# Second layer's pairs: a step's lists behind its second product on TensorE, and the pair's sum ahead of the lists' sums on VectorE

## The reference

```
x = layernorm(x + attention0(x));  x = layernorm(x + experts0(x))    # 8 experts, each takes its 256 best tokens
x = layernorm(x + attention1(x));  x = layernorm(x + experts1(x))
def experts1(x):                   # w1: 16 experts x 512 x 128, w2: 16 x 128 x 512
    logits = -sum((x[:, :, None, :] - keys) ** 2, -1) + einsum('bld,ed->ble', x, rw) + rb
    topv, topi = top_k(logits, 4);  w = softmax(topv)
    hidden = gelu(einsum('bld,efd->blef', x, w1) + b1, approximate=False)
    exp_out = einsum('blef,edf->bled', hidden, w2) + b2
    return sum(w[..., None] * take_along_axis(exp_out, topi[..., None], axis=2), axis=2)
```

## Time and profile before

| | us |
|---|---|
| median of three runs | 627.19 (625.79 to 628.24) |
| the profiled execution, its own time | 627.36 |
| span of its trace | 625.5 |
| PE busy | 541.5 (87%) |
| ACT busy | 418.0 (67%) |
| DVE busy | 438.8 (70%) |
| POOL busy | 322.7 (52%) |

### The profile page before, as it was taken

How to read it: one execution, slowest core, us unless ns; L and a number is a source line. 1 busy time by engine, 2 the same in 40 slices (tenths; PEclk the granted TensorE clock), 3 DMA queues, 4 the chain that set the end, 5 groups by cost and what they waited for, 6 DMA issues and landing times.

```text
span 625.5 us, 16615 instructions
## 1 busy us (share of the span) xinstructions
PE 541.5 (87%) x5152; PEld 382.4 (61%) x5152; DVE 438.8 (70%) x1591; ACT 418.0 (67%) x1111; POOL 322.7 (52%) x429
## 2 busy tenths in 40 slices
PE   5579999999967995279999999987999999999960
PEld 2134444545755895244455544665899999999960
DVE  5478888994486521756799999497887788743275
ACT  2138888886261564163888988732778888899834
POOL 2675666506001678465144430646566777777740
PEclk9559999999999999575999999999999999999975
DMA  6602090002100225409405000102122211211363
GB/s 194 171 25 78 12 276 3 2 2 51 21 4 4 49 48 99 146 22 273 145 10 144 3 2 2 51 19 45 49 55 54 63 59 59 60 59 58 100 202 122
DMA packets 54649, 44.42 MB, mean 71 GB/s; under 512 B 15155, under 2 KB 45123, under 8 KB 54438
## 3 DMA queue, kind: packets, MB, share of 16 engines
q1 hardware_dynamic: 47302, 31.75, 17.6%
q0 software_dynamic: 7264, 11.62, 7.2%
HBM read 29.91 MB, written 11.87 MB: 67 GB/s over the span
## 4 chain that ended last, share of the span: by engine, by line
PE 67%; DVE 11%; DMA 5%; ACT 5%; issue 5%; SPq 3%; POOL 2%; DVEq 0%; ACTq 0%; POOLq 0%
PE bank L1321 11%; PE bank L1331 10%; PE bank L905 10%; PE bank L888 7%; PE bank L870 5%; PE bank L922 3%; ACT prob L1464 2%; PE bank L1116 2%; DVE W L1964 2%; PE bank L1128 2%; PE bank L946 2%; DMA sum<-rt,idx_s 1%; PE bank L1011 1%; PE bank L930 1%; DMA prob<-xs,idx_g 1%
## 5 line engine op out<-in xcount | busy, mean ns | idle before, releaser
L1771 DVE TENSOR_REDUCE mx<-bank 128x2 f32<-128x512 f32 x256 | 163.4, 686 | 38.2 <-PE bank L870 36.4
L1464 ACT ACTIVATE prob<-bank 128x512 f32<-128x512 f32 x256 | 142.1, 601 | 36.0 <-PE bank L888 31.2
L1650 ACT ACTIVATE queries<-bank,prob 128x128 f32<-128x128 f32 x316 | 90.1, 368 | 19.5 <-PE bank L1321 16.3
L1321 PE MATMUL bank<-keys,prob 128*128 x632 | 85.5, 279 | 0.7 <-issue 0.5
L1331 PE MATMUL bank<-W,queries 128*128 x632 | 84.4, 277 | 0.0
L870 PE MATMUL bank<-keys,queries 32*128 32x256 f16 x512 | 77.9, 293 | 4.2 <-DVE mx L1771 2.0
L905 PE MATMUL bank<-prob,augs 128*32 128x256 f32 x1024 | 79.0, 393 | 0.0
L1321 PEld LDWEIGHTS bank<-keys,prob 128*128 128x128 f32 x632 | 76.8, 192 | 3.4 <-issue 2.1
L784 POOL DMA_INDIRECT prob<-xs,idx_g x64 | 61.8, 966 | 32.6 <-DVE idx_g L2175 15.5
L1331 PEld LDWEIGHTS bank<-W,queries 128*128 128x128 f32 x632 | 76.7, 192 | 1.9 <-issue 0.5
L793 POOL DMA_INDIRECT parts<-augs,idx_s x64 | 63.0, 985 | 20.5 <-issue 8.9
(11 more groups left out here) (296 smaller groups left out, 1035.8 us busy)
## 6 DMA issues: line engine op xcount, KB each, us to landing
W<-in_w SPq DMA_DIRECT2D x48, 256.0 KB, 3.8
sum<-zero SPq DMA_DIRECT2D x3, 1024.0 KB, 9.8
xr<-XT SPq DMA_DIRECT2D x12, 128.0 KB, 2.0
xs<-X SPq DMA_DIRECT2D x2, 768.0 KB, 5.5
prob<-xs,idx_g POOLq DMA_INDIRECT x80, 2.6
XB<-sum SPq DMA_DIRECT2D x1, 1024.0 KB, 5.3
Y<-sum SPq DMA_DIRECT2D x4, 256.0 KB, 4.7
W<-sum SPq DMA_DIRECT2D x4, 256.0 KB, 5.4
```

The source lines that it names most:

```text
L1321: last = nc.tensor.matmul(bank[2 + p % 2][:, P * f:P * f + P], wc[:, p % 4, P * f:P * f + P], xsT2[:, bass.ds(at, 1), :], start=True, stop ...
L1464: nc.scalar.activation(prob[:, v % 8, :, :], st_bank(b, v)[:, :], ACT.Exp, scale=SCALE).then_inc(exp_done, 1)
L1650: last = nc.scalar.activation(hid2[:, p % 4, f, :], bank[2 + p % 2][:, P * f:P * f + P], ACT.Gelu, bias=wc[:, p % 4, WB + f:WB + f + 1])
L1771: nc.vector.tensor_reduce(m_at, bank[S1B[u % 2]][:, :].rearrange("p (j k) -> p j k", j=2), AX.X, ALU.max).then_inc(s1_used, 1)
```

## The change

On PE the lists of a step stand behind its second product, and no longer ahead of it. The wait of a list on `row_ready` is gone. The registers of the next pair (expert and slot) are asked for right behind the first product, ahead of the turns. On DVE the step begins with `row_owned`, the clearing, `pair_gated` and `pair_sum`, and then come `row_listed` and the next step's `row_indicator`.

```diff
             def row_list_of(t):
                 pe.wait_ge(row_ind, t + 1)
-                if t >= 2:
-                    pe.wait_ge(row_ready, t - 1)
                 nc.tensor.matmul(bank[4 + t % 2][:, 0:2 * P + 2], ind[:, t % 2, :], RH[:, :], start=True,
                                  stop=True).then_inc(row_list, 1)
-            def pair_first(e, p):
-                at = pair_slot(pe, e, p)
+            def pair_first(at, p):
                 pe.wait_ge(rows_in, min(p + 1, NJT[1]))
...
-                expert = {}
+                expert = {0: pair_expert(pe, words, 0)}
+                slot = {0: pair_slot(pe, expert[0], 0)}
                 for p in range(NPAIR + 2):
                     if p < NPAIR:
-                        expert[p] = pair_expert(pe, words, p)
-                        pair_first(expert[p], p)
+                        pair_first(slot.pop(p), p)
                     if p == 0:
                         fill(5)
+                    if p + 1 < NPAIR:
+                        expert[p + 1] = pair_expert(pe, words, p + 1)
+                        slot[p + 1] = pair_slot(pe, expert[p + 1], p + 1)
                     for t in TURNS[p]:
                         row_turn(t)
-                    for t in LISTS[p]:
-                        row_list_of(t)
                     if p < 2:
                         fill((6, 4)[p], 7)
                     if p >= 2:
                         pair_second(expert.pop(p - 2), p - 2)
+                    for t in LISTS[p]:
+                        row_list_of(t)
...
                 for p in range(NPAIR + 2):
-                    for t in LISTS[p]:
-                        row_listed(t)
-                    for t in LISTS[p + 1]:
-                        row_indicator(t)
                     for t in TURNS[p]:
                         row_owned(t)
                     if RING <= p + 1 < NJT[1]:
                         slot_cleared(p + 1)
                     if p >= 2:
                         e = pair_expert(dve, words, p - 2)
                         s = pair_slot(dve, e, p - 2)
                         pair_gated(e, s, p - 2)
                         pair_sum(s, p - 2)
+                    for t in LISTS[p]:
+                        row_listed(t)
+                    for t in LISTS[p + 1]:
+                        row_indicator(t)
                     if p == 3:
                         count_tiles()
```

## The result

| | before | after |
|---|---|---|
| median | 627.72 (4 runs, 625.79 to 629.25) | 635.68 (4 runs, 633.89 to 636.38) |
| ratio | | 1.012, 95% interval 1.0095 to 1.0145 |
| profiled execution, span | 627.36, 625.5 | 636.38, 634.5 |
| first product of pair 0 starts at | 435.10 | 437.02 |
| steps 2 to 16 | 33.94 | 36.91 |

So the change costs 8.0 us by the medians. The two profiled executions lie 9.0 apart, and 1.9 of that is there before the first pair starts, in a part of the program that is the same in both. The 64.57 of the earlier trace rows ends at a matmul start of 544.53, but the loads of that product start at 544.26, as the first matmul records are missing there; 64.31 is the better number, and the stretches of the experiments are taken from loads.

What follows compares the result with a forecast made beforehand. POOL's full queue of indirect DMAs from scatter 0 was taken to bound the kernel. PE's 8.6 us of lateness less 2.15 slack gave 6.4: 627.36 + 6.4 = 633.8, less 0.17 to the median, 633.6 us; range 627.0 to 637.5.

Steps and rivals of the forecast that it cites:

- The removed wait at 0: Dropping PE's row_ready wait ahead of each list: at most 0.21 us per list, taken as 0.
- That the registers are not fetched earlier: Next pair's registers on PE: the instructions stay directly at the first product despite the earlier text, so 0.
- The two-list loop: Steps 2 to 16, sum through lists to sum over two steps: 5.26 us a round, 36.8 against 33.94.
- The 0.2 us by which step 2 starts earlier: Step 2's second product on PE starts 0.2 us earlier, as its two lists no longer stand ahead of it.
- Nothing from step 16 to 18: Step 17 has no list, so PE's lateness of 2.9 us is carried unchanged to step 18.
- POOL's start: Gather 32 waits for list 32, counted behind step 18's sum: 1.2 us plus PE's 2.9, so 4.1 late.
- The one-list loop: Steps 18 to 50, same loop with one list a step: 4.39 us per two steps, 70.2 against 64.57.
- The slack of 2.15 us: At the last scatters on POOL, PE's sums could be 2.15 us late before scatter 61 has to wait.
- The end: Last scatters and DVE's last addition: scatter 61, and with it the kernel's end, comes 6.4 us later.
- the first of the signs: In the profile after, PE's list loads idle for DVE's indicator in nearly every step with lists.
- the two terms (0.30 + 0.71): In both loops: 0.30 us from indicator's start to list load on PE, 0.71 from list to next first product.
- the rival that the register operations run ahead of a waiting list: On PE, list to first product takes only 0.21 us, giving 627.8, no change; chance 0.17.

Runs made afterwards that it cites:

- p2: The changed kernel with second-layer indirect transfers replaced by plain ones, indicators ahead of counts and the row_ready wait restored: 641.27 us, +1.8 to p0.
- p1: The changed kernel with the second layer's indirect transfers replaced by plain transfers of fixed rows on SP: 648.27 us, +8.8 to p0.
- p4: As p0, but with DVE's order of the change alone, PE keeping its old order: 682.67 us, +43.2 to p0.
- b0: The kernel before, unaltered, profiled on a slower chip: steps 2 to 16 took 44.13 us and steps 18 to 50 took 102.65.
- a0: The changed kernel, unaltered, against the kernel before on a slower chip: 702.51 against 702.84 us, ratio 1.000.
- p0: The kernel before with the second layer's indirect transfers replaced by plain transfers of fixed rows on SP: 639.44 us.
- p3: As p1, but with DVE's order of before, so only PE's part of the change: 641.46 us, +2.0 to p0.
- e2: The change with PE's old order, so DVE's new order alone, against the kernel before on a slower chip: 706.06 us, ratio 1.018.
- e3: Both new orders in steps 0 to 17 alone, the old ones from step 18, against the kernel before on a slower chip: 700.43 us, ratio 1.009.

## Why the prediction was right, step by step

The forecast was 633.6 us (627.0 to 637.5), and the measured median is 635.68: right in the direction and in the cause, and 2 us short in size.

- The removed wait at 0: not tried by itself. Nothing in the sums asks for more. `p2` shows that the reason given holds only for the change's own order on DVE: with the indicators ahead of the counts the same wait binds. That the registers are not fetched earlier: the 0.71 us between list and first product is there, and the trace has the register operations in it.
- The two-list loop, 36.8 us from step 2 to 16: measured 36.91, and 36.94 in `p1`. The 0.2 us by which step 2 starts earlier was taken off the stretch, where it belongs to the lateness alone: the loops give 37.0 for the stretch. Counted from the first product of pair 0, PE is 2.7 us late at step 16, where I said 2.9.
- Nothing from step 16 to 18: this was wrong by 0.4 us. The second products of the two steps are 4.87 us apart in after and 4.44 before. What costs it was not looked into.
- POOL's start, 4.1 us late at gather 32: measured 4.5.
- The one-list loop, 4.39 us for two steps and 70.2 us from step 18 to 50: the median over two steps is 4.38 in after and the stretch 70.42; 69.90 in `p1`.
- The slack of 2.15 us at the last scatters: the second product of step 50 loads at 555.42 - 437.02 = 118.40 behind the first product of pair 0, against 544.26 - 435.10 = 109.16, so 9.24 late, and scatter 61 is 7.05 late. The difference is 2.2. The forecast's 8.6 - 2.15 = 6.4 was short by the 0.6 us that PE was later than worked out: 0.2 at step 18, and 0.4 from there to step 50, of which 0.26 because the stretch before was taken as 64.57 and not 64.31.
- The end: 6.4 forecast, 7.0 to 7.1 at the last scatters and the last addition, and 8.0 between the medians. The remaining microsecond is of the size of the spread of the runs (2.5 us between the four of after) and of the 1.9 us by which the two profiles differ ahead of the pairs, so I do not explain it. In the profiles themselves the account closes: 9.2 us of lateness less 2.2 of slack, plus the 1.9 ahead of the pairs, are 8.9 of the 9.0 between the spans.
- Wrong was the first of the signs I named. PE's list should have been idle for the indicator in nearly every step with a list; it was in three steps of the early stretch and in none of the late. The loop goes through the register operations behind the list, which are held by the list's wait, and not through the list's load, which in the late steps is later than its release because the second product is ahead of it. The sum of the two terms (0.30 + 0.71) is the same either way, 0.98 measured, so the number survived the wrong picture. That is luck in part: the price of 0.71 came from one place with filling matmuls in it, and the two pictures have the same sum. For the same reason the first products of the late steps follow their list by 0.30 us in the median and not by 0.7. `p4` is the kernel that has that sign.

On the rival that the register operations run ahead of a waiting list, from the Trainium skill (Perfetto Trace Analysis, the Tensor Engine Instruction): it fell. They started when the list's semaphore was there (0.40 us behind the indicator's start in 24 of 32 late steps), and they fill the gap of 0.61 us behind the list at 446.65. What the list does not hold them up for is PE itself: at 512.05 it loads half a microsecond after its indicator, and the first product follows 0.47 us later, not 0.71. So a part of that rule is borne out: an instruction whose semaphore has come but whose engine is busy lets the sequencer go on.

## What to carry to other kernels

Before moving an instruction that waits, follow the chain through every engine until it meets itself and count how many steps it spans; its length over that number, set against what the busiest engine needs for a step, told both stretches of this change to 1% and a late step of `p4` to 3%. A wait that costs nothing in one order can close the loop in another, as `row_ready` did in `p2`. Two moves can only be judged together: here one costs 2 us, the other 43, and both 9. And when a chip disturbs the run, take out what it disturbs and compare the rest by stretches: the late stretch told the theories apart to half a microsecond, where whole times on the disturbed chips hid a change of 8 us.

## What the runs showed of the hardware that was not expected

Three of the chips needed 695 to 703 us for a kernel that took 627 on the first. Most of the loss lies in the second layer's pairs, while POOL issues indirect transfers (10 us of it from step 2 to 16 and 38 from step 18 to 50 in `b0`): what PE had finished was seen by ACT and DVE up to several microseconds late (45 of 79 first products by more than 0.6 us in `b0`, 29 in `a0`), and several releases then came together. With plain transfers from SP it was 1 of 79 in each of `p0` to `p4`, on two of these three chips, as on the first chip, and `p0` took 639 us where the kernel before took 702. Whether the indirect form or POOL's issuing delays the releases, and why not on the first chip, stays open.

On such a chip the change as a whole does not show: it is at 1.000 (0.997 to 1.003) there and at 1.012 on the first. Other orders do: DVE's part alone is at 1.018 (`e2`), and the change in the early steps alone at 1.009 (`e3`), although early and late together are at 1.000. Why the two do not add up is not explained.
